# Band attention of a two-layer decoder: the projections and values of all passes but the first as three single-pass products

## The reference, cut to what matters

```python
def _L0_attn_ref(h, q_w, q_b, k_w, k_b, v_w, v_b, pk_w, pk_b, pv_w, pv_b):
    # LOOKBACK, TOPK, CHUNK = 64, 16, 32
    q = h @ q_w.T + q_b
    k = h @ k_w.T + k_b
    v = h @ v_w.T + v_b
    ph = _phrase_states(h)            # running mean within chunks of 32
    pk = ph @ pk_w.T + pk_b
    pv = ph @ pv_w.T + pv_b
    # scores of the 64 tokens before, top 16 of them, the token before, the phrase state before
    ...
    all_sc = jnp.concatenate([seq_score[..., None], top_sc, phr_score[..., None]], axis=-1)
    all_v = jnp.concatenate([v_prev[:, :, None, :], sem_v, pv_prev[:, :, None, :]], axis=2)
    w = jax.nn.softmax(all_sc, axis=-1)
    out = jnp.einsum('bsn,bsnd->bsd', w, all_v)
    return jnp.where(t_idx[None, :, None] > 0, out, jnp.zeros((), out.dtype))

x = x + _L0_attn_ref(_layernorm(x, axis=-1), ...)
```

## Time and profile before

| | |
|---|---|
| median of three runs | 3063.18 us (3059.32 to 3067.64) |
| profiled execution, its own time | 3062.61 us |
| its span | 3060.4 us |
| band attention, with its loads | from the start to about 283.7 us |
| one pass of its loop | 31.54 us, of which PE is busy 30.54 us |
| mean granted TensorE clock over the span | 0.965 of full speed |

### The profile page before, as it was taken

The page is one execution under the profiler, slowest core; times in us unless marked ns, Lnnn a source line. Parts: engine busy times, 40 slices in busy tenths (PEclk is TensorE's granted clock), DMA queues, the critical chain, the costliest instruction groups (busy, mean ns, idle before and its releaser), DMA issues. The chain is left out here.

```text
span 3060.4 us, 48476 instructions
## 1 busy us (share of the span) xinstructions
PE 2812.1 (92%) x16477; PEld 1621.0 (53%) x16493; DVE 1832.4 (60%) x2981; ACT 1399.4 (46%) x2136; POOL 1008.3 (33%) x793
## 2 busy tenths in 40 slices
PE   7997899999968899999999999999889999859998
PEld 4554333333325555555555555555444555458998
DVE  4665667676758766657575757575545555452222
ACT  2333466666668743434343434343345555432222
POOL 1122332323036343434343434343343333051111
PEclk9998799999979999999999999999989999959999
DMA  5001222222111000000000000000043232156565
GB/s 157 0 0 45 69 58 54 60 54 59 34 56 42 1 1 1 0 0 0 0 0 0 0 0 0 0 0 1 1 118 78 68 75 63 36 182 211 192 202 170
DMA packets 102928, 159.71 MB, mean 52 GB/s; under 512 B 28349, under 2 KB 63432, under 8 KB 97160
## 3 DMA queue, kind: packets, MB, share of 16 engines
q1 hardware_dynamic: 97784, 147.88, 16.7%
q0 software_dynamic: 3408, 8.46, 0.8%
q10 hardware_dynamic: 1600, 1.61, 0.2%
HBM read 91.79 MB, written 14.96 MB: 35 GB/s over the span
## 5 line engine op out<-in xcount | busy, mean ns | idle before, releaser
L1669 DVE TENSOR_REDUCE self_nmax<-self_SM 128x2 f32<-128x1024 f32 x256 | 313.8, 1226 | 186.8 <-PE self_SM L1566 180.2
L520 DVE TENSOR_REDUCE cross_nmax<-cross_S 128x2 f32<-128x1024 f32 x256 | 312.0, 1224 | 150.7 <-PE cross_S L345 149.8
L1647 ACT ACTIVATE self_PT<-self_ST 128x1024 f32<-128x1024 f32 x256 | 262.5, 1025 | 217.5 <-PE self_ST L1589 217.4
L1707 POOL TENSOR_TENSOR self_U<-self_PT 128x1024 f32<-128x1024 f32 x64 | 153.0, 2390 | 627.3 <-ACT self_PT L1647 627.3
L1710 POOL TENSOR_TENSOR self_U<-self_U,self_PT 128x1024 f32<-128x1024 f32 x128 | 304.1, 2376 | 56.5 <-ACT self_PT L1647 52.3
L454 ACT ACTIVATE cross_PT<-cross_S 128x1024 f32<-128x1024 f32 x256 | 260.9, 1026 | 117.0 <-PE cross_S L356 116.2
L1184 DVE TENSOR_REDUCE cross_nmax<-cross_S 128x4 f32<-128x1024 f32 x128 | 156.7, 1224 | 144.4 <-PE cross_S L982 144.4
L1599 PE MATMUL self_OP<-self_PT,self_V 128*64 128x512 f32 x1024 | 233.8, 598 | 10.0 <-ACT self_PT L1647 10.0
L1683 DVE RECIPROCAL self_rcp<-self_W 128x512 f32<-128x512 f32 x64 | 214.1, 3345 | 10.1 <-PE self_W L1606 10.1
L1110 ACT ACTIVATE cross_PT<-cross_S 128x1024 f32<-128x1024 f32 x128 | 131.1, 1024 | 121.3 <-PE cross_S L998 121.3
L2905 PE MATMUL experts_AT<-experts_xT,experts_W 128*128 128x128 f32 x1280 | 153.0, 279 | 6.8 <-issue 3.7
(11 more groups left out here) (407 smaller groups left out, 5923.6 us busy)
## 6 DMA issues: line engine op xcount, KB each, us to landing
experts_W<-in_L_ffn_W SPq DMA_DIRECT2D x42, 1024.0 KB, 4.8
cross_ks<-cross_parts SPq DMA_DIRECT2D x384, 64.0 KB, 2.3
cross_qs<-cross_parts SPq DMA_DIRECT2D x376, 64.0 KB, 2.3
cross_cT<-in_ctx_T SPq DMA_DIRECT2D x16, 512.0 KB, 4.5
moe_W<-in_L_ffn_W SPq DMA_DIRECT2D x8, 1024.0 KB, 12.3
sorted_rows<-all_spare_row SPq DMA_DIRECT2D x1, 5460.0 KB, 23.9
experts_xs<-sorted_rows SPq DMA_DIRECT2D x42, 130.0 KB
experts_rest<-sorted_rows SPq DMA_DIRECT2D x41, 130.0 KB, 2.1
```

Source lines behind the costliest of these rows:

```text
L520: dve.tensor_reduce(nmax[:, g % 2, 0:R, n % PER_G], S[:, slot[st], :, :], AX.X, ALU.max, negate=True).then_inc(s_maxed, 1)
L1647: act.activation(PT[:, k, :, :], ST[:, :, :], ACT.Exp).then_inc(exped.sem, 1)
L1669: dve.tensor_reduce(nmax[:, i, 0:P:D], SM[:, :, :], AX.X, ALU.max, negate=True).then_inc(maxed.sem, 1)
L1707: pool.tensor_tensor(U[:, c % 2, :, :], PT[:, 0, :, :], PT[:, 1, :, :], ALU.add).then_inc(added.sem, 1)
```

## The change

The weights get a high part (float32r) and a remainder (weight less high part, also float32r), made once by POOL ahead of its first steps. Each `norm` step makes the same of `hT`: ACT copies the PSUM bank twice, to `hT_hi` and to `hT`, and POOL subtracts to give `hT_lo`. In all passes but the first, a projection or value product of fp32 becomes high x high, plus high x remainder, plus remainder x high, in three matmuls. `proj` 0 starts with the four matmuls that need no `hT_lo`, and then waits for both of POOL's subtractions.

```diff
+        w3_hi, w3_lo = s.sb("w3_hi", [P, KC, 3 * C], F32R), s.sb("w3_lo", [P, KC, 3 * C], F32R)
+        wvv_hi, wvv_lo = s.sb("wvv_hi", [P, KC, 2 * C], F32R), s.sb("wvv_lo", [P, KC, 2 * C], F32R)
+        hT_hi, hT_lo = s.sb("hT_hi", [P, KC, T], F32R), s.sb("hT_lo", [P, KC, T], F32R)
...
+        s_weights, lowered = s.sem("weights"), Loop(s.sem("lowered"), KC, KC)
...
-                    for c in range(KC):
-                        m = pe.matmul(dst, w3[:, c, n * P:(n + 1) * P], hT[:, c, :], start=(c == 0), stop=(c == KC - 1))
+                    if b is None:
+                        for c in range(KC):
+                            m = pe.matmul(dst, w3[:, c, cols], hT[:, c, :], start=(c == 0), stop=(c == KC - 1))
+                    else:
+                        for c in range(KC):
+                            pe.matmul(dst, w3_hi[:, c, cols], hT_hi[:, c, :], start=(c == 0), stop=False)
+                            pe.matmul(dst, w3_lo[:, c, cols], hT_hi[:, c, :], start=False, stop=False)
+                        if n == 0:
+                            lowered.wait(pe, b, 0)
+                        for c in range(KC):
+                            m = pe.matmul(dst, w3_hi[:, c, cols], hT_lo[:, c, :], start=False, stop=(c == KC - 1))
...
-                        m = pe.matmul(dst, hT[:, c, n * P:(n + 1) * P], wvv[:, c, :], start=(c == 0), stop=(c == KC - 1))
+                        if b is None:
+                            m = pe.matmul(dst, hT[:, c, cols], wvv[:, c, :], start=(c == 0), stop=(c == KC - 1))
+                        else:
+                            pe.matmul(dst, hT_hi[:, c, cols], wvv_hi[:, c, :], start=(c == 0), stop=False)
+                            pe.matmul(dst, hT_hi[:, c, cols], wvv_lo[:, c, :], start=False, stop=False)
+                            m = pe.matmul(dst, hT_lo[:, c, cols], wvv_hi[:, c, :], start=False, stop=(c == KC - 1))
...
                 elif kind == "norm":
+                    act.copy(hT_hi[:, n, :], src)
                     act.copy(hT[:, n, :], src).then_inc(done, 1)
...
+                elif kind == "norm":
+                    ring.wait_drained(pool, b, (kind, n))
+                    pool.tensor_tensor(hT_lo[:, n, :], hT[:, n, :], hT_hi[:, n, :].bitcast(F32), ALU.subtract).then_inc(lowered.sem, 1)
...
+                pe.wait_ge(s_weights, 4)
...
             @block.gpsimd
             def _(pool):
+                pool.wait_ge(s_load, 16 * N_LOADS)
+                for high, whole in ((w3_hi, w3), (wvv_hi, wvv)):
+                    pool.tensor_copy(high[:, :, :], whole[:, :, :]).then_inc(s_weights, 1)
+                pool.wait_ge(s_weights, 2)
+                for low, high, whole in ((w3_lo, w3_hi, w3), (wvv_lo, wvv_hi, wvv)):
+                    pool.tensor_tensor(low[:, :, :], whole[:, :, :], high[:, :, :].bitcast(F32), ALU.subtract).then_inc(s_weights, 1)
                 gpsimd_steps(pool, None, starting, first_ring)
-                for sem in (rooted, biased):
+                for sem in (rooted, biased, lowered):
```

More of the change, by code:

```diff
@@ L1941, in tensor_steps @@
                         ring.wait_drained(pe, b, ("norm", KC - 1), -1)
-                    dst = ring.free_bank(pe, b, (kind, n))
-                    for c in range(KC):
-                        m = pe.matmul(dst, w3[:, c, n * P:(n + 1) * P], hT[:, c, :], start=(c == 0), stop=(c == KC - 1))
+                    dst, cols = ring.free_bank(pe, b, (kind, n)), slice(n * P, (n + 1) * P)
+                    if b is None:
[9 more added lines that the diff above has]
+                            m = pe.matmul(dst, w3_hi[:, c, cols], hT_lo[:, c, :], start=False, stop=(c == KC - 1))
                     m.then_inc(ring.full.sem, 1)
                 elif kind == "v":
-                    dst = ring.free_bank(pe, b, (kind, n))
+                    dst, cols = ring.free_bank(pe, b, (kind, n)), slice(n * P, (n + 1) * P)
                     for c in range(KC):
-                        m = pe.matmul(dst, hT[:, c, n * P:(n + 1) * P], wvv[:, c, :], start=(c == 0), stop=(c == KC - 1))
+                        if b is None:
[4 more added lines that the diff above has]
+                            m = pe.matmul(dst, hT_lo[:, c, cols], wvv_hi[:, c, :], start=False, stop=(c == KC - 1))
                     m.then_inc(ring.full.sem, 1)
```

## The result

The changed kernel takes 3041.64 us (median of 4 runs, 3040.46 to 3045.37) against 3061.25 us for the kernel before (4 runs, the three of its table above among them). The ratio is 0.9938, 95% interval 0.9924 to 0.9951: 19.6 us less, with 17.9 forecast, and clear of 0.3%. The execution that was profiled is the slowest of the four, 3045.37 us with a span of 3043.6, so whole spans say little here; lengths inside the loop, which repeat to 0.05 us from its third pass on, say more.

What follows compares the result with a forecast made beforehand. PE was taken to set the pass, busy 30.54 of 31.54 us. Savings of 3.36 us a pass, less edges 0.36 and POOL wait (0.1 first, 0.5 in the other six), gave 17.9 us off 3062.6: 3045, range 3039 to 3053.

Steps and rivals of the forecast that it cites:

- signs of being wrong: In the profile after: steps over 0.25 us, a POOL wait above 1 us, or PE awaiting DVE's x update over 0.3.
- The products: Projections and values on PE: 20 products a pass, each 0.168 us shorter as three matmuls, saving 3.36 us.
- The edges: Slower first and last steps of PE's single-pass matmul runs, two runs a pass: 0.36 us lost, bounds 0 and 0.6.
- The weight loads: Loads for PE's three matmuls: taken as hidden at 0.230 us a step, though the skill's rule gives 1.01 against 0.858.
- The rival that they come to light: Projections and values: unhidden weight loads make each matmul 0.31 us, 13.6 us slower in all, 3076; chance 4%.
- The wait for POOL: In `proj` 0 after four matmuls, PE waits for POOL's subtractions: 0.5 us a pass, bounds 0 and 1.2.
- DVE's chain: Second `weigh` and x update up to the bank `out` 2 needs: slack 0.74 to about 0.2 us, no cost, at most 0.3.
- what PE gained more here DVE would take back: Ahead of `out` 2: if PE gained another 0.2 us, DVE would take it back.
- The first iteration: First changed loop pass: 3.36 less 0.36 edges and a POOL wait of only 0.1, so 2.9 us gained.
- the start and `ending`: POOL's weight work at the start and ACT's two extra copies (1 us) in `ending`: both hidden, cost nothing.

Runs made afterwards that it cites:

- run with two terms: Changed kernel with the loop's matmuls on `hT_lo` left out (20 of 60 in a pass); the pass fell by 1.8 us at best, to 27.01 us.
- POOL late: Changed kernel with each of POOL's two subtractions done twice, the first into an unread buffer; pass 31.15 us in most passes, against 28.85.

## Why the prediction was right

Time and sign were right, 3045 against 3041.6, and so was the mechanism that brings the gain: the products' fp32 records replaced by single-pass steps on the engine that set the pass before. That the sum for a pass came so close, 2.5 us forecast and 2.69 measured, is in part luck: as time of PE its terms measure 3.51 - 0.06 - 0.38 - 0.38 us, where it had 3.36 - 0.36 - 0.5 - 0, and the errors cancel. One of its signs of being wrong did come, PE waiting for DVE's x update by more than 0.3 us: it waits 0.69.

- **The products.** Forecast 3.36 us a pass, measured 3.51: the step is 0.228 us (60 of them, 13.7 us, for 17.16 before) where I took 0.230.
- **The edges.** Forecast 0.36 us, measured under 0.1 for the two runs of a pass. Scores and values together take 8.08 us, the scores' 2.58 and 24 steps of 0.228 are 8.05; scores and projections take 10.80 us where the wait for POOL is gone, for 2.58 and 36 steps, 10.77. The edges that I had read beside the self attention's matmuls don't come back beside these.
- **The weight loads.** The rival that they come to light didn't happen. The Trainium skill ("TensorE: Matmul & The Clock Gate", Part 3, The mechanism) has a load overlap only with matmuls on other rows; this case's trace doesn't agree: a pass has 60 full-height loads of 0.19 us, one for each matmul, and 54 of the distances between those matmuls are 0.224 to 0.236 us. The same section's bracket about a background weight buffer, in the paragraph ahead of that list, is what fits.
- **The wait for POOL.** Forecast 0.5 us. Measured are 0.26 over a step, and 0.38 with the slower step behind it, which is what the projections lose by holding the matmuls back (8.89 to 8.51 us). The times of ACT and POOL that it was worked out from held to 0.25 us. But in the changed kernel it costs nothing: the pass is 28.87 without it.
- **DVE's chain.** This is the step that failed, though time and sign came out right: "So that slack falls from 0.74 to about 0.2 us: no cost taken, 0.3 as upper bound." PE waits 0.38 us more before `out` 2, over the bound, and this wait closes the loop that sets the pass, 28.85 us where PE needs 28.08 with both waits gone. With S the start of the projections, as there, PE wants the bank at S + 13.67 (13.7 forecast), but DVE frees it at S + 13.84 (13.5 forecast). I had tied DVE's chain to projection 3's eviction and moved it up with the faster projections. In the kernel before the second `weigh` did wait for that; in the changed one it is ready in time, and the chain is the 14.56 us since the scores of tile 2, which no faster projection moves. The sentence that what PE gained more here DVE would take back was the right one, and it was true already of the whole wait for POOL, not only from another 0.2 us on.
- **The first iteration** gave 3.4 us instead of 2.9 (31.64 to 28.20; the forecast of 28.6 had counted from 31.54), the wait for POOL being nothing there; from the loop's first projection to the cross attention the gain is 19.06 us, for 17.9 forecast. What the start and `ending` changed by can't be told from scatter.

## What to carry to other kernels

When an engine that is busy 97% of a loop gets faster, the next bound need not be an engine that is busy all the time: DVE has work for only 73% of the pass here. It can be the loop of buffers and results that two engines close between them; follow it once round, from event to event, for what doesn't move with the edit. Two waits in series on one engine aren't two costs: take either away and the other may grow by the same amount, so price them by taking out both, and by breaking what closes the loop. Work with a late deadline (here statistics of 1.9 us) doesn't belong between a result and the buffer that it frees, even where that costs nothing today.

## What the runs showed of the hardware that was not expected

PE's idle time was followed by a lower clock in some passes and not in others. In the run with two terms PE waits 2.6 to 3.1 us before `out` 2 in every pass, and four of seven passes have a longer `out` stretch behind it. Windows of that run, two behind a wait of 3.04 us that ended at 169.28, one of the stretch after them, and one behind a wait of 3.03 us that ended at 115.23:

```profile
169.30:176.60 7.30, 7.30 (x19) 5.80 (x20) 3.38 (x9) 0.00 (x0) 0.27 (x1) 0.59 0.00 0
170.00:175.00 5.00, 5.00 (x14) 3.94 (x13) 2.23 (x6) 0.00 (x0) 0.00 (x0) 0.50 0.00 0
176.60:180.00 3.40, 3.40 (x14) 2.32 (x13) 2.70 (x13) 0.54 (x1) 0.00 (x0) 1.00 0.00 0
115.30:118.70 3.40, 3.40 (x16) 3.01 (x17) 2.84 (x8) 0.00 (x0) 0.23 (x1) 1.00 0.00 0
```

Behind the first wait the granted clock is at 0.50 of full speed, the level of 1.2 GHz (0.59 as a mean over 7.3 us), and at full speed behind that; behind the other, equal wait it stays at 2.4 GHz. The lower clock costs 1.6 to 2.9 us in a pass of this run. With POOL late it came in two of seven passes, behind a wait of 1.95 us in the first and one of 2.56 in the fifth; behind the other five waits, of 2.56 to 2.58 us, it didn't. In the loops of the other runs, whose waits on PE are 1.25 us or less, it came in none. What decides between two equal waits no run here shows.
